# Start-up loads in another order, seven of them issued by ScalarE, and an order table with many steps moved by a few places

## What is computed

```python
x = x + L0_xattn(layernorm(x), ctx)   # x0: 16 heads of 8, softmax over the tokens of x
x = x + L0_ffn(layernorm(x))          # f0: self-attention, 8 heads of 64, values and outputs
                                      #     from 2 of 5 experts, chosen by top-2
x = x + L1_xattn(layernorm(x), ctx)   # x1: one head of 128, only the 32 largest scores kept
x = x + L1_ffn(layernorm(x))          # f1: causal attention, 16 heads of 8 with 4 key heads;
                                      # m1: mixture of 8 experts of 128x128, top-2
x = x + L2_xattn(layernorm(x), ctx)   # x2: one head, no weights
x = x + L2_ffn(layernorm(x))          # gated, quantised to 8 bits, scale from the maximum of all x
x = x + L3_xattn(layernorm(x), ctx)   # x3: 16 heads of 8, causal
x = x + L3_ffn(layernorm(x))          # f3: 128 -> 512 -> 128 with relu
```

## Time and profile before

| | us |
|---|---|
| three runs | 1533.61, 1545.13, 1547.38 (median 1545.13) |
| the profiled execution, its own time | 1541.52 |
| its span in the profile | 1539.8 |
| PE busy | 1263.7 (82%) |
| DVE busy | 1075.6 (70%) |
| ACT busy | 848.8 (55%) |
| POOL busy | 806.1 (52%) |
| mean granted clock of PE | 0.899 |

### The profile page before, as it was taken

How to read it: one execution, slowest core, us unless ns; L and a number is a source line. 1 busy time by engine, 2 the same in 40 slices (tenths; PEclk the granted TensorE clock), 3 DMA queues, 4 the chain that set the end, 5 groups by cost and what they waited for, 6 DMA issues and landing times. The chain is left out here.

```text
span 1539.8 us, 37252 instructions
## 1 busy us (share of the span) xinstructions
PE 1263.7 (82%) x14512; PEld 974.3 (63%) x14513; DVE 1075.6 (70%) x2505; ACT 848.8 (55%) x2715; POOL 806.1 (52%) x822
## 2 busy tenths in 40 slices
PE   3788888987888888787898788789885588899997
PEld 2567676674767666566667657557473366667776
DVE  2467687787877687877678788976555887655652
ACT  1788666455458548657848646544534333445542
POOL 2039498496477438742964855873223423334342
PEclk9598787998979889999999899999987677999999
DMA  6000000000000000000000000001010000000000
GB/s 155 6 6 2 1 2 1 2 2 1 21 1 1 20 2 1 2 21 2 1 21 2 1 1 10 8 9 45 1 56 19 1 1 2 9 10 9 16 9 15
DMA packets 26695, 19.06 MB, mean 12 GB/s; under 512 B 6520, under 2 KB 24216, under 8 KB 26392
## 3 DMA queue, kind: packets, MB, share of 16 engines
q1 hardware_dynamic: 26520, 16.67, 3.7%
HBM read 12.73 MB, written 3.93 MB: 11 GB/s over the span
## 5 line engine op out<-in xcount | busy, mean ns | idle before, releaser
L1201 ACT ACTIVATE arena<-bank 128x512 f32<-128x512 f32 (+5 forms) x361 | 186.1, 546 | 251.4 <-PE bank L507 69.3
L1602 DVE TENSOR_REDUCE arena<-pair 128x8 f32<-128x1024 f32 (+2 forms) x224 | 241.1, 1096 | 102.4 <-PE pair L557 43.7
L2222 POOL TENSOR_SCALAR_AFFINE_SELECT arena<-arena 128x1024 f32<-128x1024 f32 (+1 forms) x128 | 143.3, 1133 | 295.1 <-ACT arena L1571 157.0
L2277 POOL TENSOR_TENSOR arena<-arena 128x512 f32<-128x512 f32 x160 | 189.0, 1181 | 49.9 <-DVE arena L1719 43.3
L1248 ACT ACTIVATE arena<-pair,arena 77x128 f32<-77x128 f32 x512 | 178.2, 370 | 35.3 <-DVE arena L1602 25.0
L2282 POOL TENSOR_TENSOR arena<-arena 128x512 f32<-128x512 f32 x128 | 178.3, 1393 | 10.0
L502 PE MATMUL bank<-ident 128*128 128x128 f32 x780 | 128.3, 306 | 9.5 <-POOL subscale L2174 4.3
L502 PEld LDWEIGHTS bank<-ident 128*128 128x128 f32 x780 | 112.0, 214 | 26.6 <-issue 10.8
L2298 POOL TENSOR_TENSOR arena<-arena 128x512 f32<-128x512 f32 x64 | 67.6, 1069 | 115.8 <-ACT arena L1201 73.8
L1571 ACT ACTIVATE arena<-pair 77x1024 f32<-77x1024 f32 x64 | 62.3, 1014 | 105.5 <-PE pair L1126 100.5
L1248 ACT ACTIVATION_READ_ACCUMULATOR arena<-pair,arena 77x1 f32 x512 | 108.8, 212 | 0.0
(11 more groups left out here) (294 smaller groups left out, 3062.7 us busy)
## 6 DMA issues: line engine op xcount, KB each, us to landing
arena<-in_ctx_turned SPq DMA_DIRECT2D x16, 154.0 KB, 2.5
arena<-in_x SPq DMA_DIRECT2D x8, 256.0 KB, 5.5
out<-arena SPq DMA_DIRECT2D x8, 256.0 KB, 2.3
spill<-arena SPq DMA_DIRECT2D x7, 256.0 KB, 2.0
arena<-spill SPq DMA_DIRECT2D x7, 256.0 KB, 4.5
arena<-in_ctx SPq DMA_DIRECT2D x8, 154.0 KB
arena<-in_ctx_turned SPq DMA_DIRECT2D x1, 1232.0 KB, 5.8
wexp<-in_L_ffn_expert_w SPq DMA_DIRECT2D x1, 512.0 KB, 4.5
```

The costliest lines, as they stand in the source:

```text
L1201: return act.activation(dst, src, func, bias=bias, scale=scale)
L1602: return dve.tensor_reduce(dst, src, X, op, **kw)
L2222: return pool.affine_select(out=e, in_=e, compare_op=ALU.is_ge, fill=0.0, base=0, pattern=[[0, 8], [1, 128]], channel_multiplier=-1)
L2277: pool.tensor_tensor(into, xvs[:, b, ex * SHD:(ex + 1) * SHD].unsqueeze(1).broadcast_to([128, SH, SHD]), gates[g % 2][:, b, 0:SH, ex].unsq ...
```

## The change

Three things change. The seven loads of f0 are issued by ACT, ahead of everything else that ACT does. SP issues the rest in another order: x and context of group 0, the loads x0, x and context of group 1, x1, the other context of group 0, x of group 2, f1, x of group 3, the other context of group 1, then b, then x of groups 4 to 7. And the strings of `ORDER` for stages A and C have steps moved; the strings of stage B and the table `FILL` are as they were. Two of the lines of the table stand for the rest here.

```diff
@@ -37,58 +37,58 @@
     ("A", "tensor"):
-        "wiawwwwiwawawwabbwbbwwcbbcbbcaacacabdbbddddecbbeeecbeffbeeebcffaeeageaacffechbhfbgbbfcbhchdbgddbbdcd"
+        "awwwaaabbiwiwwwwwbbwwwcbbcbbcaacacabdbdbdddbecbeecbeeffbeeecbffeeaageacfeafchbhfbgbbfcbhchdbgdddbbec"
...
@@ -1197,6 +1197,9 @@
 
         @block.scalar
         def _(act):
+            for dst, src in LOADS["f0"]:
+                act.dma_start(dst, src).then_inc(loaded["f0"], 16)
+
             def copy(dst, src, bias=0.0, scale=1.0, func=ACT.Identity):
                 return act.activation(dst, src, func, bias=bias, scale=scale)
 
@@ -2429,19 +2432,24 @@
+            def load(name):
+                for dst, src in LOADS[name]:
+                    sp.dma_start(dst, src).then_inc(loaded[name], 16)
+
             load_x(0)
             load_ctx0(0)
-            for name in ("x0", "f0"):
-                for dst, src in LOADS[name]:
-                    sp.dma_start(dst, src).then_inc(loaded[name], 16)
+            load("x0")
             load_x(1)
             load_ctx0(1)
-            for name in ("b", "x1", "f1"):
-                for dst, src in LOADS[name]:
-                    sp.dma_start(dst, src).then_inc(loaded[name], 16)
-            for g in range(NCTX):
+            load("x1")
+            load_ctx(0)
+            load_x(2)
+            load("f1")
+            load_x(3)
+            for g in range(1, NCTX):
                 load_ctx(g)
-            for g in range(2, NG):
+            load("b")
+            for g in range(4, NG):
                 load_x(g)
```

More of the change, by code:

```diff
@@ L39 @@
     ("A", "tensor"):
-        "wiawwwwiwawawwabbwbbwwcbbcbbcaacacabdbbddddecbbeeecbeffbeeebcffaeeageaacffechbhfbgbbfcbhchdbgddbbdcd"
[L41 to L47, removed]
+        "awwwaaabbiwiwwwwwbbwwwcbbcbbcaacacabdbdbdddbecbeecbeeffbeeecbffeeaageacfeafchbhfbgbbfcbhchdbgdddbbec"
+        "dheahaeeaegceefacfbehfhfbbgeeiebicbhfihfgeibicffbiihhbicgjdjjjckhdhlkgcdldldkhhmkeellemelfeifleiiefl"
+        "mefgeiiemmeihfhefgnnfnjfnnjhjjnhkngndnknldnhdllhdnknmlgnknlllmdmhilneiehmeaeamaeaiinbbiffengnenenini"
+        "nbhhinfbnfbjcjgjenjneechbhnffnbegcnbnfiifkhnclhckagaladddlakhdlmhdlkmlieiblimeleembemiefeficibennefe"
+        "fnbejjgbfnjnjfnnhechgnnfknnfbhlbhnglnkcmnbhhlngkcillicnkhmlaaahldamlididibdmdbemiebieicnenbnfbfjenje"
+        "ncejbnnefbjnnfgnenecebnffenhhcngcnkflkfinlhilhaakdamkgaldlbbdmddhbhegebeceehclhbbffmibileiecfefgebie"
+        "eihchlifgcmefjjmjjdffhknhlngldndkddnnmknhlnelnlnhekmnnglleennmlefnefenmffmhhiigneenenefniifhinnnenhg"
+        "iifnnifhnnhgjnjnjjnknhhlkgllnkmhiilhlkmilliyyyiymlyyyyyyymyimiiyynynnyjjjjknnklnnnnllknmnllkmnllnmnl"
         "nmmnnnnnnnnnnnnnnnnn",
@@ L51 @@
     ("C", "tensor"):
-        "ababcbdcabddceaddcecaddceaddcebbadedceddfcefffdfdcaeddfcedebdcbedfdffcedffdcfdedcedbedcbedfdcfefdfdf"
-        "ceddfcebddebceddfceffdfdfceddfcedebdcbedfdcffeddffcfdedcebdedbceddfcedffdfcefddfcededcedfdfffdedfdef"
+        "ababcbdcabddceadcdecaddceaddcedbbaedceddfffcffeddacedfdcedebcbdedffdfcfeddfcfdedcedbedbceddffcfefddf"
+        "cedfdcebddebceddcfdeffdcffddefcebddecbedfdcfeffddfcfdedcedbdebceddfcedfdfcfefdfdcededcedfdfffdedfdef"
         "eeffffff",
     ("A", "scalar"):
[L56 to L62, removed]
+        "awwawaiwbbwwwwwbwbwwbbbbccaccaabdbdddbedbedcbfecfebbfefcefbfeaagfcefahffbbgfbfbhcbdcbgddbddehcedaabe"
+        "fgeefcaffhfebfbgbeifecihfbgifbiffibcfihbcjjgbdjjchdgllddhddeellflelefiiffflieeflgiifeehfngffnfjnjfnn"
+        "jhjnngdnnndnhldldnnllnglldnihlndleeaeaaeifnibfbfignenneniinnhfbnnfjfjbgcjjnnebechfnbffnbgncfbfinhnfc"
+        "gadalldaddhlldliilebledlifeeibfieffecnbfnefjjefngjfnnfjbnhnfgcbnnfnfnhbbgnllnnchbgcnlilnhalaldaillid"
+        "ddibdeeibdibncffnejjfnebjnnbejcfnnfennfbbgnncfeenfbhnffcngnffinhlladagldaldbddhbebgecbfehlcledffbibi"
+        "bfifecegfeibfheicllgffjjfjjfdhfnglnddlndnndnnhdelnlennngllnfnelfenleffffhnginenfeeififnnnhninngiffin"
+        "nfhnngjnjjnjnhngllnhilliliyylilyyyyylyyyyyiiyynjynjyjjnnnnnllnnnllnnllnnllnnnnnnnnnnnnnnnnnn",
     ("B", "scalar"):
@@ L90 @@
     ("C", "gpsimd"):
-        "bbddbddddddddfddfddbddddfbddddfddddfddddfdbdddfddbddfddddfddddfbddddfdddddfdddfddfddddff",
+        "bbdddbdddddddfbdfdddddddfddddbfddddfddddbddfdddfddfdddbddffdddbdddddfddddfddddfddddddfff",
 }
```

34 lines of the change are left out of this document (17 added, 17 removed).

## The result

The changed kernel took **1560.3 us** (median of 4 runs, 1558.9 to 1563.8); the kernel before, beside it on the same chip, 1545.7. The ratio on record is 1.0125, 95% interval 1.0084 to 1.0167; the two medians themselves lie 14.6 us apart, 0.94%. Single runs more than 1.5% above the fastest of their kernel (in experiments 3, 9 and 12 and in the kernel before) are left out of the ratios, though not out of the medians. The forecast was 1532, 1510 to 1552. The profiled execution took 1559.06 us (span 1557.3), 17.5 us above the profiled one of before, and that is what the trace has to explain.

A forecast was written before the change was run, and what follows sets the result against it. The start was taken as a closable gap behind a 19.0 us context-load wait, the rest as a tight weave with no engine full. 1541.5 - 12.7 + 0 for the table = 1528.8, plus 3.6 to the median: 1532 us, range 1510 to 1552.

The forecast's parts named there:

- The start: Opening of the kernel: new loads and table head end the 19.0 us context wait, gaining 12.7 us; alone 1532, chance 0.45.
- u4's exponentials: ACT's exponentials for score unit u4, in the start: to begin at 46.5 us instead of 59.16.
- b was in: Start: b's last load, w_down, usable at 26.8 us instead of 16.7; DVE's quantisation through at 38.4.
- Stages B and C unchanged: After stage A: B and C keep their 362 us within 3.
- The rest of the table, cost 0: Moved steps beyond the start, mostly stage A: costed at 0, with ends of -18.5 and +37 us from PE's idle time.
- a filled hole on VectorE: Stage A, group 3's maximum amax moved before 786.42 us: 0.67 us out of a full stretch into a 2.69 us hole.
- Slower: late drains: Rival, stage A: late ACT drains of PSUM banks hold PE; decided by PE idle over 198 us; 1569 us, chance 0.10.
- The table closes holes: Rival, throughout stage A: moved steps fill idle time, a tenth of PE's idle gives 1514 us; chance 0.27.

The follow-up runs named there:

- experiment 3: Changed kernel with the tables of before on all four engines for TensorE steps 369 to 550 of stage A: 1551.0 us, ratio 1.0048 to the kernel before.
- experiment 9: Changed kernel's loads and tables up to about 190 us, then the order of before to the end, stage C included: 1533.4 us, ratio 0.9936 to the kernel before.
- experiment 12: Kernel before with its own loads, but the head of the changed tables up to about 190 us: 1541.9 us, ratio 0.9999 to the kernel before.
- experiment 1: Changed kernel's loads and head of tables up to about 90 us, then the tables of before to the end: 1533.3 us, ratio 0.9937 to the kernel before.
- experiment 2: Changed kernel with stage C's tables of before: 1559.2 us, ratio 1.0104 to the kernel before.
- experiment 4: Changed kernel with the tables of before on all four engines for TensorE steps 670 to 721 of stage A: 1550.0 us, ratio 1.0042 to the kernel before.
- experiment 10: Changed kernel with the tables of before from about 190 to 552 us (TensorE steps 112 to 369): 1552.8 us, ratio 1.0050 to the kernel before.
- Experiment 17: Kernel before with two GpSimd gate products moved ahead of group 3's first f0 difference, filling a 6.00 us wait: 1539.8 us, ratio 0.9993.
- experiment 7: Changed kernel with VectorE's 3.2 us maximum of f0's group 7 put back behind two gate steps of group 5: 1559.6 us, ratio 1.0092 to the kernel before.
- experiment 18: Changed kernel with GpSimd's first f0 difference of group 3 and the gate product moved ahead of it exchanged back: 1562.6 us, ratio 1.0134 to the kernel before.
- experiment 5: Changed kernel with GpSimd's two moved group-7 steps (LayerNorm of x0, bias addition) put back behind those of group 6: 1552.4 us, ratio 1.0053 to the kernel before.

## Why the prediction was wrong

- **The start: right.** Reckoned 12.7 us from u4's exponentials, measured 11.3 at u4's maximum, 9 at step 38, and 10 in the time of experiments 1 and 9. b was in 0.7 us later than reckoned, and its quantisation done 1.5 later. The clock in 46 to 78 us was 0.63 instead of 0.50.
- **Stages B and C unchanged: right.** From the end of A the profiled execution took 1.8 us less than before, and experiment 2 found no difference.
- **"The rest of the table, cost 0": wrong, and it is the whole miss.** It costs 27 us by experiment 1 against the changed kernel, and experiments 3, 4 and 10 find it in three stretches of A. The step that failed is the sentence "These places save work that nobody waited for directly", from which this term was put at 0. I asked of a moved step who waits for *it*, and with an answer of "nobody soon" took it as free. At its new place it holds what stands behind it in the list; that is shown for one step, in the middle stretch. GpSimd's moves of groups 6 and 7 were in front of me; I named the bias addition (15 places) and passed over the LayerNorm step next to it (17 places, 5.4 us), which stands directly ahead of the reciprocal root of group 3. And I looked closely at only one place, a filled hole on VectorE, where 344 steps had moved.
- **The range.** The ends of that term were set unevenly by feeling, -18.5 and +37, and then the upper one was given 0.10. Two readings of before would have spoken for more weight on the slow side (an argument, not tested by itself): PE, DVE, ACT and POOL are each busy 59% to 83% of A, so that a late step finds little slack on its way, and at the lower clock scores take 1.99 us instead of 1.10. The sum with the measured terms is 1541.5 - 10 + 27 = 1558.5, and the profiled execution took 1559.1; that is no independent check, since the 27 comes from the same medians.
- **The rivals.** "Slower: late drains" had the right sign. Its point, PE's idle time in A over 198 us, was passed: from 60 to 1197 us, where A now ends, PE is busy 933.1 of 1137 us and idle 203.9, against 185.3. But what starts the wait read in the middle stretch is no late drain of a PSUM bank. It is GpSimd's list. Right sign, another mechanism.
- **"The table closes holes"** (0.27): it does close some. Experiment 17 closes one of 6 us on GpSimd and gains nothing that shows.

Still open: which moves make the early and the late stretch longer, and why PE's clock is lower in the middle and the late one. The experiments show that restoring a stretch gives 8 to 10 us each time, that neither VectorE's moves nor those of the other three together carry the early one, and that the single exchanges tried (experiments 7 and 18) do not. Not tried is SyncE's new order with f0's loads left to it, so what ScalarE's issuing is worth within the 10 us of the start is not known.

## What to carry to other kernels

In a hand-ordered program ask two questions of every moved step: who waits for it, and who stands behind it now. In the changed kernel the second was worth 8 us, for two steps of which the long one took 5.4 us and was not needed for another 33; in the kernel before the same move cost nothing that shows, so the price depends on the rest of the order. Where the order was settled over the whole length, take the part of a change that has a measured gain (here the loads with the head of the tables) and leave the rest as it was: cut at a place where both orders have done the same steps.

## What the hardware showed

**VectorE beside GpSimd.** The 88 products of 128x32 elements with two operands in SBUF take 191 to 194 ns when no GpSimd tensor operation runs beside them (40 of them before, 25 in the changed kernel) and up to 1.30 us when one does. All 88 together take 33 to 35 us in the order of before (6 kernels) and 39 to 45 in the changed one (10). DVE and POOL in the changed kernel, group 5:

```profile
996.30 1.05 DVE L1681 TENSOR_TENSOR arena<-arena 128x32 f32<-128x32 f32 x1
997.38 0.98 DVE L1683 TENSOR_TENSOR arena<-arena,rank 128x32 f32<-128x32 f32 x1
998.40 0.19 DVE L1605 TENSOR_REDUCE arena<-arena 128x4 f32<-128x32 f32 x1
998.62 0.88 DVE L1688 TENSOR_TENSOR arena<-arena 128x32 f32<-128x32 f32 x1
```

```profile
995.79 1.51 POOL L2319 TENSOR_TENSOR arena<-arena,b1o 128x512 f32<-128x512 f32 x1
997.26 2.19 POOL L2280 TENSOR_TENSOR arena<-arena 128x512 f32<-128x512 f32 x2
```

The reduction between them, with one operand, keeps its 0.19 us. The Trainium skill, page "SBUF — State Buffer", section "SBUF: two separate sides", says that VectorE and GpSimd share one pair of ports as an exclusive lock, which a VectorE instruction with two SBUF inputs needs too, against a GpSimd operation that reads SBUF. The rows agree: each small product ends about when a GpSimd operation does. GpSimd pays as well: the two operations of its reciprocal root took 1.53 and 2.71 us at 755 us, beside VectorE products of 1280, 640 and 320 columns, and 0.23 and 1.03 at 763 us. Experiment 17 made such an overlap and experiment 18 took one away; over the whole kernel nothing shows.

**Waits and the lower clock.** Behind PE's wait of 4.73 us the next products ran at the lower of the two levels, 1.2 GHz: granted 0.72 over those 24 us. In experiment 5 it stood from 755 to 763 us, behind a wait of 2.42. But the length of the wait does not decide. In the kernel before, PE waited 3.40 us at 974.4 us for GpSimd's LayerNorm, and the clock stayed at 1.00. In experiment 9 the lower level came at 764 us behind waits of 0.96 and 0.29, and in the changed kernel at 974 us behind one of 1.06. What decides is open. Its price can be read: the late stretch has PE busy for 54.0 us at 1.00 and 62.1 us at 0.87, with the same 431 products. It also moves single profiles: in kernels with the order of before, the middle stretch took 121 to 129 us.
